# Feed-forward biases added by GpSimd instead of multiplied in on TensorE, and the nodes of layer 1 shifted block by block

## What is computed

```python
# layer 0 (h = normalised x, gains and shifts g, b)
h = ln(x, g1, b1); q, k, v = h @ Wq + bq, h @ Wk + bk, h @ Wv + bv
alpha = softmax over the edges of a target of (q[dst] * k[src]).sum(-1) / 4
x1 = x + segment_sum(alpha * v[src]) @ Wo + bo
L0 = x1 + gelu(ln(x1, g2, b2) @ W1 + bf1) @ W2 + bf2
x = layernorm(x + L0)
# layer 1 (k and v of an edge get e = edge_attr @ We)
conv = segment_sum(alpha * (v[src] + e)) + x @ Wskip + bskip
h = ln(conv + x, g1, b1)
L1 = ln(gelu(h @ Wf1 + bf1) @ Wf2 + bf2 + h, g2, b2)
out = layernorm(x + L1)
```

## Time and profile before

| | us |
|---|---|
| median of 3 runs | 1449.92 |
| lowest and highest run | 1449.18, 1460.9 |
| the profiled execution | 1454.89 |
| its span, first to last instruction | 1452.7 |

### The profile page before, as it was taken

The page is one execution under the profiler, slowest core; times in us unless marked ns, Lnnn a source line. Parts: engine busy times, 40 slices in busy tenths (PEclk is TensorE's granted clock), DMA queues, the critical chain, the costliest instruction groups (busy, mean ns, idle before and its releaser), DMA issues. The chain is left out here.

```text
span 1452.7 us, 28509 instructions
## 1 busy us (share of the span) xinstructions
PE 1087.0 (75%) x6861; PEld 962.0 (66%) x6861; DVE 1080.6 (74%) x2695; ACT 841.0 (58%) x2605; POOL 895.7 (62%) x995
## 2 busy tenths in 40 slices
PE   3937778777777778679995788877887887776790
PEld 1436678677776777659635687777777876675680
DVE  5538778777787778854444888888889888888447
ACT  1615766677666766635441566676667666755351
POOL 2077777777777777420017777777777777780543
PEclk9968777777777777769997899999999999987795
DMA  5285555555555555400024666665666567650001
GB/s 154 87 184 179 162 190 193 190 161 181 190 194 174 164 194 190 153 32 0 12 83 146 204 192 203 219 204 191 205 219 203 190 206 226 199 189 15 1 0 44
DMA packets 100515, 222.36 MB, mean 153 GB/s; under 512 B 34860, under 2 KB 49739, under 8 KB 96798
## 3 DMA queue, kind: packets, MB, share of 16 engines
q0 software_dynamic: 39936, 109.11, 25.3%
q1 hardware_dynamic: 57927, 109.78, 22.0%
q10 hardware_dynamic: 2518, 1.92, 0.4%
HBM read 184.73 MB, written 36.00 MB: 152 GB/s over the span
## 5 line engine op out<-in xcount | busy, mean ns | idle before, releaser
L458 POOL DMA_INDIRECT KV<-kv_table,idx x832 | 818.4, 984 | 322.4 <-issue 307.9
L725 PE MATMUL PS<-QT,OHT 128*128 x1664 | 404.5, 332 | 172.4 <-DVE OHT L984 135.2
L725 PEld LDWEIGHTS PS<-QT,OHT 128*128 128x128 f32 x1664 | 320.5, 238 | 192.6 <-issue 191.2
L726 PE MATMUL PS<-QT,OHT 128*128 x1664 | 389.7, 323 | 0.0
L726 PEld LDWEIGHTS PS<-QT,OHT 128*128 128x128 f32 x1664 | 320.1, 239 | 0.0
L585 ACT ACTIVATE AGG<-AGG,PC,RCS x800 | 309.3, 387 | 2.5 <-ACT AGG L581 1.8
L1002 DVE TENSOR_TENSOR PR<-KV,PS 128x512 f32<-128x512 f32 x208 | 140.5, 675 | 108.4 <-DMA KV<-kv_table,idx 106.6
L771 PE MATMUL PS<-OH,KV 128*128 128x128 f32 x1600 | 206.1, 278 | 3.4 <-DVE OH L1104 1.2
L581 ACT ACTIVATE AGG<-PS 128x127 f32 x800 | 207.9, 260 | 1.0 <-issue 0.7
L771 PEld LDWEIGHTS PS<-OH,KV 128*128 128x128 f32 x1600 | 193.7, 194 | 6.2 <-issue 3.1
L995 DVE TENSOR_TENSOR KV<-KV,PS 128x1024 f32<-128x1024 f32 x104 | 125.6, 1207 | 80.6 <-DMA KV<-kv_table,idx 54.1
(11 more groups left out here) (158 smaller groups left out, 1368.8 us busy)
## 6 DMA issues: line engine op xcount, KB each, us to landing
REL<-rel_dram SPq DMA_DIRECT2D x52, 512.0 KB, 4.5
window_dram<-OH SPq DMA_DIRECT2D x25, 1024.0 KB
OH<-window_dram SPq DMA_DIRECT2D x50, 512.0 KB, 5.4
KV<-kv_table,idx POOLq DMA_INDIRECT x832
EA<-in_edge_batch SPq DMA_DIRECT2D x52, 256.0 KB, 3.2
kv_table<-KV SPq DMA_DIRECT2D x52, 128.0 KB, 1.7
X<-in_x SPq DMA_DIRECT2D x2, 832.0 KB, 9.9
GATES<-edge_gates SPq DMA_DIRECT2D x8, 208.0 KB, 9.4
```

Source lines behind the costliest of these rows:

```text
L458: g.indirect_dma_start(KV[:, s, j, :], None, kv_table, bass.IndirectOffsetOnAxis(ap=idx[:, s, j:j + 1], axis=0)).then_inc(gathered[s][hh], 16)
L725: te.matmul(o, OHT[:, q // 2, 0, e0:e0 + P], QT[:, ds(blk, P)], start=True, stop=False)
L726: last = te.matmul(o, OHT[:, q // 2, 1, e0:e0 + P], QT[:, ds(blk + P, P)], start=False, stop=True)
```

## The change

The two feed-forward biases are loaded once more, as FB: each of the 128 partitions gets both rows. Layer 1's row has its first shift b1 added (`fb_made`), so that the second of `affine`'s two additions brings in both. In layer 0 GpSimd follows each quad's addition (now counted by `x_pair`) by one that adds the bias row to the quad. `narrow` starts with its first float32 product. The last two blocks of columns are no longer split into bfloat16 parts. The addition of b2 to X is made per block, behind `keep`, in layer 1's projection, four blocks later than the copy, once VectorE has added the unshifted block into Y.

```diff
-        bf2 = [BIAS[:, (8 + l) * D:(9 + l) * D] for l in range(2)]
+        FB = sb("FB", [P, 2, D])
@@ GpSimd
             pool.wait_ge(S["weights_loaded"], 16 * WEIGHTS)
+            g.tensor_tensor(FB[:, 1, :], FB[:, 1, :], GB[:, 1, :], ALU.add).then_inc(S["fb_made"], 1)
@@ GpSimd, layer 1's projection
-                    blocks(pool, keep)
+                    def shift(n, k):
+                        pool.wait_ge(*done("batch_step", n + 1))
+                        pool.sem_inc(S["pool_go"], 1)
+                        g.tensor_tensor(X[:, ds(n * P, P)], X[:, ds(n * P, P)], GB[:, 3, :], ALU.add).then_inc(S["x_shifted"], 1)
+
+                    pipelined(pool, (keep, 4), (shift, 0))
@@ GpSimd, behind the gathers
-                if l:
-
-                    x3 = X[:, :].rearrange("p (n d) -> p n d", n=NB)
-                    g.tensor_tensor(x3, x3, GB[:, 3, :].unsqueeze(1).broadcast_to([P, NB, D]), ALU.add).then_inc(S["x_shifted"], 1)
-
@@ GpSimd, layer 0's quads
-                        g.tensor_tensor(X[:, at], X[:, at], Y[:, at], ALU.add).then_inc(S["x_summed"], w)
+                        g.tensor_tensor(X[:, at], X[:, at], Y[:, at], ALU.add).then_inc(S["x_pair"], w)
+                        pool.wait_ge(*done("x_pair", b + w))
+                        pool.sem_inc(S["pool_go"], 1)
+                        x3 = X[:, at].rearrange("p (b d) -> p b d", b=w)
+                        g.tensor_tensor(x3, x3, FB[:, 0, :].unsqueeze(1).broadcast_to([P, w, D]), ALU.add).then_inc(S["x_summed"], w)
                 else:
+                    pool.wait_ge(*done("fb_made", 1))
@@ GpSimd, affine
-                        g.tensor_tensor(Y[:, at], Y[:, at], GB[:, 1, :], ALU.add).then_inc(S["ln_affine"], 1)
+                        g.tensor_tensor(Y[:, at], Y[:, at], FB[:, 1, :], ALU.add).then_inc(S["ln_affine"], 1)
@@ ScalarE, before the load of GB (WEIGHTS goes from 11 to 12)
+            w(FB[:, :, :].rearrange("p a d -> p (a d)"), row(a["biases"][8 * D:10 * D]).broadcast_to([P, 2 * D]))
@@ TensorE, narrow
-                    te.matmul(o, ones3[:, :], bf2[l], start=True, stop=False)
                     for c in range(4):
-                        last = te.matmul(o, gT[k][:, c, :], W2[l][:, c, :], start=False, stop=(c == 3))
+                        last = te.matmul(o, gT[k][:, c, :], W2[l][:, c, :], start=(c == 0), stop=(c == 3))
@@ VectorE
-                    split_biases(3, 10)
+                    split_biases(3, 8)
-            dve.wait_ge(*done("x_shifted", 1))
+            dve.wait_ge(*done("x_shifted", NB))
```

More of the change, by code:

```diff
@@ L184, in build @@
             alpha_done rc_done rcd_done at_ready rce_ready rcs_ready oh_ready pv_ready agg_ready
-            pc_ready act_col count_turned ga_ready last_oh_ready last_copy last_col
+            pc_ready act_col count_turned ga_ready last_oh_ready last_copy last_col fb_made x_pair
             """.split()
@@ L1319 @@
 FIRST_WEIGHTS = 3
-WEIGHTS = 11
+WEIGHTS = 12
 _SHAPED = ["L0_gnn_Wo", "L0_gnn_W1", "L0_gnn_W2", "L1_gnn_We", "L1_gnn_Wf1", "L1_gnn_Wf2"]
```

## The result

The changed kernel takes 1420.37 us (median; 1417.5 to 1424.92) where the kernel before, measured beside it, takes 1452.28: a ratio of 0.9762 with a 95% interval of 0.9727 to 0.9798. That is 2.4% or 32 us less. Forecast were 1439.4 us, 0.7% less, and a range of 1435.0 to 1445.0. Of the 21 us missed, 11 are the bias matmul, which cost two and a half times what the forecast gave it, and 8 are the gathers, which the forecast had at nothing.

The account below looks back on a forecast made before the run. GpSimd's issue of 832 indirect gathers was taken to pace the edge rounds, TensorE the feed-forward stages. The terms -7.1 - 6.7 + 3.0 + 0.3 = -10.5 us took 1449.92 to 1439.4 us, range 1435.0 to 1445.0.

Parts of the forecast that it names:

- The bias matmul: Both feed-forward stages: without it a block falls from 2.25 to 2.11 us, -7.1 us in all, bounds 6.8 and 7.7.
- the upper bound of 0.15 a block: Feed-forward stages: at most 0.15 us saved in all 52 blocks, the whole step from L854 to L856, given as 7.7 us.
- three blocks of each stage without a saving: Feed-forward stages: the lower bound of the saving, three blocks of each stage save nothing, given as 6.8 us.
- The gathers: Edge rounds of both layers: the diff touches no gather, so the two long stretches stay as they are, 0 us.
- The long addition: End of layer 1's rounds: without GpSimd's addition, VectorE's copy falls from 6.83 to 0.13 us, -6.7 us, bounds 6.0 and 7.0.
- The moments: Layer 0, before feed-forward: VectorE's moments wait beside GpSimd's second additions, +3.0 us, bounds 0.5 and 3.9.
- The shift in the projection: Layer 1's projection: GpSimd's 26 block-wise additions just clear VectorE's next operation, +0.3 us, bounds 0 and 4.0.
- Layer 0's projection and residual: Layer 0's stages ahead of its gathers and ahead of its moments: no change in time, 0 us each.
- 1: End of layer 1's rounds is not freed, something else is late where the copy stood: 1446.1 us, chance 0.06.
- 2: Feed-forward stages: the bias matmul was hidden, ScalarE, VectorE or GpSimd sets the block: 1446.5 us, chance 0.04.
- 4: Layer 1's projection: the shift sets its pace, 26 normalisations each wait a whole addition, 11.9 us: 1451.0 us, chance 0.03.
- 3: Layer 0's moments: no contention costs, GpSimd's additions fall into gaps, other parts add a little: 1435.5 us, chance 0.15.

Follow-up runs that it names:

- e5: Kernel before with the 52 feed-forward bias matmuls taken out and nothing put in their place: 1439.39 us, ratio 0.9908.
- e3: Kernel before with only the block-by-block shift of the nodes in layer 1's projection, no long addition, bias matmuls kept: ratio 0.9956.
- e2: Changed kernel with the shift undone: biases added by GpSimd, one long addition again behind the gathers; ratio 0.9846 to the kernel before.
- e14: Changed kernel as it is, run again beside a variant without projection bias matmuls: 1788.23 us, ratio 0.9929 to the kernel before.

## Why the prediction was wrong, point by point

- **The bias matmul, -7.1 forecast, -18 measured.** This is the step that failed, and the term was mis-sized, not the mechanism. "Without a bias matmul between, eight such records and the step to the next group take 1.00 us": that 1.00 was read from L856, the group right behind the bias matmul, which had itself lost 0.10 us by it. The trace held no undisturbed step between two full groups at full clock, so the 1.00 could not be the price without it, and the upper bound of 0.15 a block was no bound. Measured: 0.89 and 0.90 for each group, 0.35 a block (e5, and the rows after). The rows of before held the hint: the eight records of L847 take 1.06 us, the eight of the same size behind the short matmul (L856) 1.16. With 0.27 for one record (L841), seven steps of L847 are 0.79 us, so eight are 0.90. The two bounds do not follow from their conditions either: 52 x 0.15 is 7.8, and three blocks of each stage without a saving leave 2 x (22 x 0.14 + 0.06) = 6.3.
- **The gathers, 0 forecast, about -8 measured.** "Nothing in the diff touches a gather, so the two long stretches should stay as they are" was right on the diff and wrong on the time: with 832 instructions in line, 10 ns each is more than the whole forecast for the bias matmul. No row of the trace pointed at it. The 8 us are the difference of the ten profiles above; what in GpSimd makes the gathers shorter stays open.
- **The long addition, -6.7 forecast, -6.2 measured** (e3), within its bounds of 6.0 to 7.0. The copy took 0.13 us as forecast. In the pair of profiles 4.4 stand, since the shorter gathers end earlier ahead of the same work (e2, with them and without the shift, has 41.30 us there, where before has 39.56 and 39.99).
- **The moments, +3.0 forecast, +3.8 measured** in the pair, just inside the bound of 3.9, and +2.4 in e2 and +2.8 in e14. Two-input operations wait as the one-input ones do (L881 and L882, 1.29 and 1.30 us). The rule of the Trainium skill used in the forecast (SBUF — State Buffer, Who interferes with whom), that the one which starts first keeps the other out for its whole instruction, agrees with these rows. GpSimd's additions reached further than forecast, though: they end 5.5 us behind the first of the moments (646.02 against 640.52), where the forecast had 3.9.
- **The shift in the projection, +0.3 forecast, 0.2 measured** by e3 (47.86 against 47.63). The 3.1 us of the pair were the clock.
- **Layer 0's projection and residual**, -3.8 and -1.4 us in the pair, are differences between executions: the changed kernel itself took 40.2 to 45.9 and 10.9 to 13.0 us in its three profiles.
- **The rivals.** 1, 2 and 4 did not come: the end of the rounds was freed, the matmul was not hidden, the projection kept its pace. 3 had the direction, not the size. No rival held that the matmul cost more than its step.

With the two wrong terms put right, the sum of the forecast is -18 - 6.2 + 3.8 + 0.2 - 8.2 = -28.4 us, against 31.9 between the medians; the remaining 3.5 us lie within the spread of these two stages.

## What to carry to other kernels

The price of a short instruction in a pipelined stream is the period with it minus the period without, and the second must come from a place where it stands neither ahead nor behind; if the trace has none, the steps seen do not bound the cost from above, and the period inside an undisturbed group is the better guide. A bias matmul of one or three rows between full ones costs 0.2 us more than its own step (0.35 us a block here with three rows, 0.61 with one), and adding the bias on VectorE or GpSimd, which had room, was cheaper at all four places here. Where one instruction recurs 800 times on the path, a change of 1% in it weighs as much as the forecast gave to all 52 bias matmuls, so the forecast needs a term for it even if the diff does not touch it.

## What the runs showed of the hardware

- A matmul of three rows (bfloat16) or one row (float32) between groups of 128 rows: 0.10 us lost on either side beside its own 0.155 and 0.41 us.
- One addition of 128 columns on GpSimd ahead of the first indirect gather: the median of the 832 gathers 7 to 11 ns shorter; a memset in its place, or the addition after 416 gathers: nothing.
- On three of the five chips of the experiments the gathered rows were taken up 28 to 45 us behind their issue instead of 2 to 17, GpSimd waited some 2.7 us for a free slot before each eighth gather, and the kernel before took 1794 to 1801 instead of 1455 to 1457 us; which gain of a change counts hung on that.
- The same code was granted TensorE's higher clock after one block of a stage or after four, worth 3 us.
